# Attention 0 of a two-layer transformer block: half of its unmasked maximum scans split into a half of the scores and a clipped difference

## The reference, cut to what matters

```python
q = apply_rope(q, 0)                      # 32 heads of 16 features
k = apply_rope(k, 0)                      # 8 key heads, each shared by 4 query heads
scores = jnp.einsum('bhqd,bhkd->bhqk', q, k) / math.sqrt(HEAD_DIM)
scores = jnp.where(causal[None, None, :, :], scores, jnp.float32(-1e+20))
attn = jax.nn.softmax(scores, axis=-1)
out = jnp.einsum('bhqk,bhkd->bhqd', attn, v)
```

## Time and profile before

| | us |
|---|---|
| median of 3 executions (lowest, highest) | 1353.01 (1350.63, 1364.93) |
| profiled execution, its own time | 1344.81 |
| its span | 1343.1 |
| TensorE busy | 1205.7 |
| VectorE busy | 953.5 |
| ScalarE busy | 671.2 |
| GpSimd busy | 375.2 |

### The profile page before, as it was taken

One profiled execution on the slowest core, in us unless ns is written; L12 is line 12 of the kernel. 1 busy time (PEld: TensorE's weight loads), 2 busy tenths in 40 slices (PEclk: granted clock), 3 DMA queues, 4 the chain that ended last, 5 costly groups with the idle time before them and its releaser, 6 DMA issues.

```text
span 1343.1 us, 21792 instructions
## 1 busy us (share of the span) xinstructions
PE 1205.7 (90%) x6800; PEld 753.2 (56%) x6800; DVE 953.5 (71%) x2990; ACT 671.2 (50%) x1023; POOL 375.2 (28%) x505
## 2 busy tenths in 40 slices
PE   4998999999899877998879999999988988879988
PEld 1875444443388865444868744444435887744368
DVE  5889889898166676653659798999962667576365
ACT  2621666666655452544436036666665554435542
POOL 0431411122254400114614323122213542002162
PEclk9996899999999997999979858999999999869999
DMA  8374411220010020100140742112200100120001
GB/s 317 120 196 87 125 29 26 57 65 3 1 49 1 1 47 19 55 2 0 63 175 23 189 130 70 26 26 57 66 2 0 50 1 17 32 72 2 1 8 56
DMA packets 37285, 76.20 MB, mean 57 GB/s; under 512 B 5084, under 2 KB 6620, under 8 KB 37036
## 3 DMA queue, kind: packets, MB, share of 16 engines
q1 hardware_dynamic: 37176, 74.82, 19.2%
HBM read 48.98 MB, written 27.08 MB: 57 GB/s over the span
## 4 chain that ended last, share of the span: by engine, by line
PE 64%; DVE 19%; issue 5%; POOL 5%; ACT 5%; DMA 1%; DVEq 0%; SPq 0%; ACTq 0%; POOLq 0%
PE bank L999 16%; PE bank L871 12%; PE bank L779 5%; PE bank L780 5%; PE bank L781 5%; DVE maxes L1208 5%; PE bank L983 4%; PE bank L977 3%; DVE unused L1204 3%; PE bank L765 3%; DVE ops L1152 3%; PE bank L881 2%; POOL x L1484 2%; POOL w_odd L1466 2%; ACT ops L1356 2%
## 5 line engine op out<-in xcount | busy, mean ns | idle before, releaser
L1431 ACT ACTIVATE probs<-bank 128x1024 f32<-128x1024 f32 (+3 forms) x416 | 367.9, 911 | 320.4 <-PE bank L983 220.3
L871 PE MATMUL bank<-ops 48*128 48x512 f32 (+3 forms) x960 | 321.8, 436 | 34.5 <-DVE maxes L1204 17.2
L1204 DVE CUSTOM_DVE_ANT_0 unused<-bank,causal 128x128 bf16<-128x128 f32 (+3 forms) x640 | 279.5, 486 | 47.7 <-PE bank L871 44.1
L1542 POOL TENSOR_SCALAR_AFFINE_SELECT probs<-probs 128x256 f32<-128x256 f32 (+1 forms) x256 | 118.8, 464 | 640.3 <-ACT probs L1431 640.0
L871 PEld LDWEIGHTS bank<-ops 48*128 48x128 f32 (+1 forms) x960 | 163.0, 206 | 218.9 <-DVE maxes L1204 96.0
L999 PE MATMUL bank<-probs,v_mem 128*17 128x512 f32 (+6 forms) x1920 | 252.2, 517 | 6.1 <-ACT heads_raw L1418 5.6
L1208 DVE TENSOR_REDUCE maxes<-bank 128x1 f32<-128x512 f32 x320 | 207.4, 684 | 40.7 <-PE bank L871 39.2
L983 PE MATMUL bank<-ops 50*128 50x512 f32 (+2 forms) x640 | 175.9, 448 | 5.0 <-ACT probs L1431 4.8
L779 PE MATMUL bank<-ops,xT 128*128 128x512 f32 (+1 forms) x288 | 116.2, 403 | 19.6 <-DVE x L1068 11.6
L983 PEld LDWEIGHTS bank<-ops 50*128 50x128 f32 x640 | 86.6, 197 | 57.9 <-ACT probs L1431 29.5
L1473 POOL TENSOR_TENSOR rstd<-var_eps,minus_half 128x1 f32<-128x1 f32 x96 | 52.7, 549 | 215.1 <-DVE var_eps L1046 214.5
(11 more groups left out here) (117 smaller groups left out, 1965.5 us busy)
## 6 DMA issues: line engine op xcount, KB each, us to landing
query_rows_dram<-ops SPq DMA_DIRECT2D x48, 256.0 KB, 3.8
ops<-query_rows_dram SPq DMA_DIRECT2D x64, 192.0 KB, 4.4
w_odd<-staging_wqkv SPq DMA_DIRECT2D x4, 1536.0 KB, 7.3
x<-x_dram SPq DMA_DIRECT2D x16, 256.0 KB, 6.1
ops<-ops SPq DMA_DIRECT2D x16, 256.0 KB, 3.0
out_dram<-x SPq DMA_DIRECT2D x16, 256.0 KB, 2.0
staging_wqkv<-wqkv_dram SPq DMA_DIRECT2D x2, 1536.0 KB, 15.8
key_rows_dram<-ops SPq DMA_DIRECT2D x24, 128.0 KB
```

The costliest lines, as they stand in the source:

```text
L871: last = mm(dst[:, h * w:(h + 1) * w], queries(a, u)[rows, t // 4, hi, t % 4 * P:(t % 4 + 1) * P], keys(a, u, hi)[rows, HALF * kp:HALF * k ...
L1204: V.tensor_tensor_reduce(unused[:, masked % 3, 0:w], part, causal[:, HALF - w:], 1.0, NEG, ALU.add, ALU.max, dst).then_inc(s["max_done"].s ...
L1431: A.activation(probs[:, e % 6, :, 0:cols], scores[:, 2 * (e % 2):2 * (e % 2) + 2, 0:cols], ACT.Exp, scale=a.scale).then_inc(s["exp"].sem, 1)
L1542: G.affine_select(out=p, in_=p, compare_op=ALU.is_ge, fill=0.0, base=0, pattern=pattern, channel_multiplier=-1).then_inc(s["masked"].sem, 1)
```

## The change

For the eight unmasked banks of a unit that belong to the first query block (`i` 0) the bank no longer holds the scores of 512 keys. Its left 256 columns hold the scores of keys 0 to 255, its right 256 columns the product with the difference of key rows, keys 256 to 511 minus keys 0 to 255. ScalarE clips the right half at zero (Relu) into one of three buffers `over`, and VectorE adds it to the left half and takes the maximum in one `tensor_tensor_reduce` of 256 columns, since max(a, b) = a + relu(b - a). The other eight unmasked banks keep their reduction of 512 columns.

Around this, the banks of a query tile are put in another order; an instruction on VectorE writes the differences into lanes 64 to 127 of the first key products, which are then stored with them (128 lanes in place of 64; the high and low parts are still made of 64 lanes); two transfers load them; TensorE waits for them ahead of such a bank; and `xT` moves into the tail of `ops` to make room. The buffers of `over` are those of `hw_mem` and `v_rest`, which the attention does not use.

```diff
+        if self.row_tiles == 2:
+
+            for t in range(4, NT):
+                at = [n for n, m in enumerate(self.max_banks) if m[0] == t]
+                first, second = ([self.max_banks[n] for n in at if self.max_banks[n][1] == kp] for kp in range(2))
+                half = len(second) // 2
+                self.max_banks[at[0]:at[-1] + 1] = first[:2] + second[:half] + first[2:] + second[half:]
...
+        self.halved = [n for n, (t, kp, w, g, diag) in enumerate(self.max_banks) if not diag and self.row_tiles == 2 and g[0][1] == 0]
...
-        xT = sb("xT", [P, 2, 2, KC, P], F32R)
-        ops = sb("ops", [P, 20, SEQ], F32R)
+        ops = sb("ops", [P, 22, SEQ], F32R)
...
+        over = [hw_mem[:, 0:2, :], hw_mem[:, 2:4, :], v_rest]
...
+            if n == 0:
+                last.then_inc(s["summed"].sem, 1)
+                eng.wait_ge(s["summed"].sem, s["summed"].at(b, 1))
+                half = HALF // 2
+                last = ops_of.tensor_tensor(prods[64:P, 0:2, 0:half], prods[0:64, 0:2, half:], prods[0:64, 0:2, 0:half], ALU.subtract)
+            last.then_inc(s["turned"].sem, 1)
...
+            def load_key_differences(b):
+                sp.wait_ge(rope_stored[0].sem, rope_stored[0].at(b, 96))
+                for r in range(2):
+                    dst = ops_flat[64 * r:64 * r + A0.part_rows, 20480:21504].bitcast(F32).rearrange("p (n s) -> p n s", n=4)
+                    sp.dma_start(dst, k_rows[8:16].rearrange("(n r) p s -> r p n s", r=2)[r, :, :, 0:HALF // 2]
+                                 ).then_inc(key_differences_done.sem, 16)
...
+                    if g == 0:
+                        load_key_differences(b)
...
+                    if n in a.halved:
+                        r, hi = heads_in[0]
+                        pe.wait_ge(key_differences_done.sem, key_differences_done.at(b, 32))
+                        rows = a.score_rows(r, a.part_rows)
+                        last = mm(dst.rearrange("p (n s) -> p n s", n=2), queries(a, u)[rows, 1, hi, t % 4 * P:(t % 4 + 1) * P],
+                                  halved_keys(u // 2)[rows], start=True, stop=True)
...
+                        elif n in a.halved:
+                            k = a.over_at[i]
+                            dve.wait_ge(s["over"].sem, s["over"].at(b, k + 1))
+                            V.tensor_tensor_reduce(unused[:, paired % 3, 0:w // 2], src[:, 0:w // 2],
+                                                   over[k % 3].rearrange("p n c -> p (n c)"), 1.0, NEG,
+                                                   ALU.add, ALU.max, dst).then_inc(s["max_done"].sem, 1)
+                            paired += 1
...
+            def clip_difference(b, st, i):
+                a, s = ATT[st], qs[st]
+                act.wait_ge(s["ring_full"].sem, s["ring_full"].at(b, i + 1))
+                A.activation(over[a.over_at[i] % 3].rearrange("p n c -> p (n c)"), ring[i % 3][:, HALF // 2:], ACT.Relu
+                             ).then_inc(s["over"].sem, 1)
...
                         for n, (_, cols) in enumerate(a.events[k_]):
                             e = u * a.unit_events + a.events_before[k_] + n
+                            if n == 1:
+                                clip_differences(ring_no + len(a.ring_at[g][0]))
                             act.wait_ge(s["scored"].sem, s["scored"].at(b, e + 1))
...
+                    clip_differences(len(a.ring_first) + sum(len(slot) for step in a.ring_at[:g + 1] for slot in step))
```

More of the change, by code:

```diff
@@ L133, in plan_max @@
                 self.max_banks += [(t, kp, w, g, diag) for g in groups]
+        if self.row_tiles == 2:
[5 more added lines that the diff above has]
+        self.halved = [n for n, (t, kp, w, g, diag) in enumerate(self.max_banks) if not diag and self.row_tiles == 2 and g[0][1] == 0]
         self.max_ops_to = list(itertools.accumulate(len(m[3]) for m in self.max_banks))
         self.unit_max_ops = self.max_ops_to[-1]
-        ops = [m[4] for m in self.max_banks for _ in m[3]]
-        self.masked_ops = [n for n, diag in enumerate(ops) if diag]
+        self.paired = [m[4] or n in self.halved for n, m in enumerate(self.max_banks)]
+        ops = [pair for m, pair in zip(self.max_banks, self.paired) for _ in m[3]]
+        self.paired_ops = [n for n, pair in enumerate(ops) if pair]
         self.max_banks_of = [sum(m[0] < 4 for m in self.max_banks), len(self.max_banks)]
@@ L235, in plan_ring @@
         self.norm_at = [i for i, item in enumerate(self.ring) if item[0] == "norm"]
+        self.over_at = {i: n for n, i in enumerate(i for i, item in enumerate(self.ring)
+                                                   if item[0] == "max" and item[2] in self.halved)}
 A0 = Attention("rot", 32, 8, 16, 0.25, 2, True, ahead=1.07, slack=12)
@@ L380, in build @@
         ops_flat = ops.rearrange("p n s -> p (n s)")
+        xT = ops_flat[:, 20480:22528].rearrange("p (m n k c) -> p m n k c", m=2, n=2, k=KC)
         regions = {"E": [ops_flat[:, 0:2048], ops_flat[:, 2048:4096]],
@@ L408, in keys, with halved_keys @@
             return ops_flat[:, first:first + 1024]
+        def halved_keys(v):
+            first, second = 64 + 4 * v, 80 + v
+            return ops_flat.rearrange("p (n s) -> p n s", s=HALF // 2)[:, first:second + 1:second - first, :]
         def all_keys(a):
@@ L442, in build @@
         keys_first_done = signal("first_keys_loaded", 32)
+        key_differences_done = signal("key_differences_loaded", 32)
         keys_second_done = signal("second_keys_loaded", 32)
@@ L488, in build @@
             s["turnable"] = signal(f"{n}_rope_products", 6)
+            s["summed"] = signal(f"{n}_first_keys_roped", 1)
             s["turned"] = signal(f"{n}_roped", 6)
@@ L496, in build @@
             s["max_done"] = signal(f"{n}_max_done", a.units * a.unit_max_ops)
+            s["over"] = signal(f"{n}_differences_clipped", a.units * len(a.halved))
             s["shift_step"] = signal(f"{n}_shift_step", 3 * a.units)
@@ L529, in rope_sums @@
             ops_of.tensor_tensor(prods[0:m, 0, :], prods[0:m, 0, :], prods[0:m, 3, :], ALU.subtract)
-            ops_of.tensor_tensor(prods[0:m, 1, :], prods[0:m, 1, :], prods[0:m, 2, :], ALU.add).then_inc(s["turned"].sem, 1)
+            last = ops_of.tensor_tensor(prods[0:m, 1, :], prods[0:m, 1, :], prods[0:m, 2, :], ALU.add)
+            if n == 0:
[4 more added lines that the diff above has]
+            last.then_inc(s["turned"].sem, 1)
         def queries_count(u):
@@ L542, in build @@
         rope_lanes = [64, P, 64, P, P, P]
+        stored_lanes = [P, P, 64, P, P, P]
         @block.sync
@@ L612, in store_rope @@
                 _, hi, lo = rope_set(n % 2)
-                lanes, rows = (64, k_rows) if keys_only else (P, q_rows[16 * (n // 4):16 * (n // 4) + 16])
+                lanes = stored_lanes[n]
+                rows = k_rows[0:lanes // 8] if keys_only else q_rows[16 * (n // 4):16 * (n // 4) + 16]
                 rows = rows.rearrange("h (p m d) s -> p m h d s", p=3, m=2)
@@ L868, in ring_item @@
                     operands_ready(b, st, u, t)
-                    for h, (r, hi) in enumerate(heads_in):
+                    if n in a.halved:
[4 more added lines that the diff above has]
+                                  halved_keys(u // 2)[rows], start=True, stop=True)
+                    for h, (r, hi) in enumerate(heads_in if n not in a.halved else ()):
                         rows = a.score_rows(r, a.part_rows)
@@ L1193, in ring_read @@
                     t, kp, w, heads_in, diag = a.max_banks[n]
-                    masked = u * len(a.masked_ops) + sum(len(m[3]) for m in a.max_banks[:n] if m[4])
+                    paired = u * len(a.paired_ops) + sum(len(m[3]) for m, pair in zip(a.max_banks[:n], a.paired) if pair)
                     for h, head in enumerate(heads_in):
@@ L1408, in attention, with clip_differences @@
                 ns = len(a.steps)
+                ring_no = max(a.begun.values())
+                def clip_differences(upto):
+                    nonlocal ring_no
+                    for i in range(ring_no, upto):
+                        if i in a.over_at:
+                            clip_difference(b, st, i)
+                    ring_no = upto
+                clip_differences(len(a.ring_first))
                 for g in range(a.units * ns + a.lag + 2):
@@ L1594 @@
     rows = [nc.dram_tensor(f"{n}_dram", shape, F32, kind="Internal").ap()
-            for n, shape in (("key_rows", (8, 48, SEQ)), ("query_rows", (32, 48, SEQ)))]
+            for n, shape in (("key_rows", (16, 48, SEQ)), ("query_rows", (32, 48, SEQ)))]
     build(nc, w.pop("x"), w, scratch, *rows, out)
```

13 lines of the change are left out of this document (6 added, 7 removed).

## The result

The changed kernel took 1443.02 us (median of 4 executions, 1439.76 to 1452.41); the kernel before, run beside it, 1355.36. The ratio is 1.0649, with a 95% interval of 1.0567 to 1.0730. The prediction was 1376 with a range to 1400: the sign was right, the size was not.

The account below looks back on a forecast made before the run. VectorE was taken to pace the ring. The profiled 1344.8 us plus 25.5 for late clips, minus 4.0 in the burst, plus 1.5 for the subtraction gave 1367.8; the same +23.0 on the median 1353.0 gave 1376 us, range 1338 to 1400.

Parts of the forecast that it names:

- What bounds the kernel: First attention, steady units: VectorE sets the ring's pace, working 26.29 of 28.26 us; it holds up TensorE, which holds up ScalarE.
- its warning: In one unit the chain of waits lies on VectorE for only 19.9%, mostly on TensorE's own queue; the margin is thin.
- the lower bound of 1322 us: Every clip is in time and only the saving of 2.0 us per unit counts: -30.5 us in all.
- The scan's spacing: VectorE's new 256-column scans start 0.35 us apart against 0.60 for plain reductions: 0.25 us saved per bank, 2.0 per unit.
- Lateness of the clips: Tiles 4 to 7: eight clips late by 5.13 us per unit; less saving and absorbed waits, +1.82 net, 14 units +25.5.
- the 1.31 us of old waits: VectorE's present waits for TensorE, 1.97 us per unit less 0.66 already counted, that can vanish into the stalls for clips.
- The stores at nothing: Storing 128 lanes and two more loads cost nothing, since tile 4 already waits for the second keys; otherwise some us per sequence.
- The burst at -4.0: First unit's eight halved banks per sequence, in the burst and step 0 with ScalarE nearly idle: 16 x 0.25 us saved.
- a rival at 0.13 and at 33 us: Steady units: TensorE standing for clips is granted a lower clock, one spell of 2.37 us per unit, 1409 us; chance 0.13.
- Clips in time: Rival: full banks ahead of VectorE hide the path through ScalarE, only the saving counts, 1322 us; chance 0.15.
- A draw: Rival: half the lateness is hidden or stalls fall where the chain lies on TensorE, about 1353 us; chance 0.22.
- The rule that relu belongs on VectorE: A skill's rule against the clip on ScalarE; relu as a second VectorE pass was put at +13 us, 1366 us.

Follow-up runs that it names:

- free scan: Changed kernel without clips or waits for them; VectorE scans the left 256 columns with zero mask columns, clipped half left out: 1339.25 us, ratio 0.9876.
- clips in the burst alone: Changed kernel with the old bank order and only the six banks per sequence ahead of the first step halved and clipped: 1353.43 us, ratio 1.0003.
- no clips: Changed kernel without ScalarE's clips and VectorE's wait for them, VectorE reducing all 512 columns; new order, difference matmuls and transfers stay: 1394.61 us, ratio 1.0284.

## Why the prediction was wrong in size

**What bounds the kernel: right, with its warning.** VectorE is the pace of the ring. The free scan shows what relief of it is worth: 0.8 us per unit for 1.75 us of work. My sum gave relief its full 2.0 us, and the lower bound of 1322 us with it.

**The scan's spacing: right, where it doesn't wait.** The new scan takes 425 ns, and neighbours start 0.35 us apart, with a float32 second operand as with the mask:

```profile
115.41 0.42 DVE L1255 CUSTOM_DVE_ANT_0 unused<-bank,hw_mem 128x256 bf16<-128x256 f32 x1 [0.33 <-ACT hw_mem L1461]
...
115.76 0.42 DVE L1255 CUSTOM_DVE_ANT_0 unused<-bank,hw_mem 128x256 bf16<-128x256 f32 x1
```

In the units, where each waits, VectorE's work fell by 1.4 us and not by 2.0.

**Lateness of the clips: right in kind, a third too small.** The two clips of tile 7 and the first of tile 4 waited 0.67, 0.76 and 0.69 us where 0.60, 0.86 and 0.63 were worked out. The last of tile 6 waited 1.39 where I "took 0.1": the step failed in that I looked only at what stands ahead of the clip on ScalarE, not at the value matmuls ahead of its bank. Together they are 7.76 against 5.13, and 2.29 of the 2.63 more fall on tiles 5 and 6, at the low clock. The net at full clock was 2.3 us per unit against 1.82, 14 x 0.5 = 7 us more in all. That the net came so near is in part luck: the lateness was larger, the work saved was less, and more than the 1.31 us of old waits was absorbed. Without the clock's 12 x 4.3 = 52 us the profiled execution would have taken some 1394 us against the 1367.8 of my sum, and these 26 us are the 7 and the places outside the steady units.

**The stores at nothing: perhaps wrong by some 2 us.** In the chain of waits after, ahead of the first ring matmul, stands a transfer where the kernel before shows none:

```profile
83.35 4.24 DMA query_rows_dram<-ops
...
87.96 6.50 DMA ops<-query_rows_dram
```

The first ring matmul, before the change and after:

```profile
91.63 0.44 PE L871 MATMUL bank<-ops 48*128 48x128 f32 x4
```

```profile
94.59 0.53 PE L917 MATMUL bank<-ops 48*128 48x128 f32 x4 [0.59 <-DMA ops<-query_rows_dram]
```

It is 3.0 us late. With the same stores it came at 92.40 (clips in the burst alone), 92.75 (free scan) and 94.08 (no clips), and in the kernel before with doubled matmuls in the burst, which has neither the subtraction nor the stores, at 92.42. So of the 3.0 us about 1 is the spread of traces, and up to 2 may be the stores in sequence 0. The cover I named (tile 4 waits anyway) was the wrong place to look: the queries of the first tiles are loaded behind these stores.

**The burst at -4.0: it gave nothing back.** The row of six units begins 9.4 us late in sequence 0 (167.5 for 158.1), with a clock of 0.53 from 106 to 140 us where it had been 0.60. By the same rows the 101 us are 9.4 ahead of the six units of sequence 0, 38.6 in them, 9.4 from there to the six of sequence 1, 41.0 in those and 2.8 behind. What of the 21.6 us outside is clock and what stalls wasn't worked out.

**The step that failed: the clock stood at nothing in the sum, held as a rival at 0.13 and at 33 us, where it was the larger half.** I argued from the end of the attention, where TensorE has less to do and keeps 1.00, that a TensorE that stands more keeps its clock. The runs say otherwise where VectorE holds it up: low clock per unit was 0.6 to 1.7 us before, 13.4 after, 10 with VectorE's scans of the halved banks doubled, and about 10 with only 1.2 us of work added. The rival had the form right, one spell of low clock in each unit; it took the spell of 6.7 us seen before, and it was 10 to 17 us. Twelve units at 0.35 x 12 us are some 50 us of the 80, the rest the stalls. Both were in my text; they are not rivals but add up, and the traces tie the one to the other: the clock falls right behind the two late clips of tile 4. The Trainium skill (TensorE: Matmul & The Clock Gate, section "A second HAM failure mode: psum-queue depth-cycling") describes a case like this, with bf16 matmuls of 512 columns: a TensorE that idles briefly and often while it cycles through PSUM banks goes back and forth between its two clocks. The trace agrees in that, with a fall and a rise in each unit and 0.81 on average in a ring of three banks. The same skill (Trainium Kernel Development and Optimization, section "Performance Expectations") calls matmul busy time a bad metric for how close a kernel is to the roofline. The trace agrees: it rose from 167.85 to 195.40 us in six units on 1156 matmuls each.

**The rivals.** Clips in time: refuted, each waits. A draw: refuted, the kernel lost 88 us. The rule that relu belongs on VectorE stayed on the right side in sign, as the clip on ScalarE made the kernel slower than before; relu on VectorE, for which I worked out 1366 us, wasn't tried, so whether it beats either is open.

**What stays open.** What in the stands brings the clock down. Standing is not the whole of it: in the kernel before the clock fell at 232.5 us behind 4 us in which TensorE was busy for 3.90, more than at tile 4, where it kept its clock.

```profile
228.50:232.50 4.00, 3.90 (x29) 2.04 (x31) 4.00 (x17) 3.76 (x5) 0.00 (x0) 1.00 0.03 6
232.50:236.50 4.00, 4.00 (x17) 1.55 (x9) 3.02 (x8) 1.54 (x2) 0.00 (x0) 0.50 0.00 0
```

The order of banks alone gave 0.91 and 0.90 in its two rows of six units, with the difference matmuls and transfers 0.89 and 0.83, at nearly one pace; the free scan, with those same matmuls, 0.98. Whether the second step is the operands or chance wasn't separated, nor why these two, with VectorE's work as before, had so much more low clock than the kernel before.

No version that computes the whole result was faster than the kernel before. The free scan was, by 1.2%, but it leaves out the clipped half.

## What to carry to other kernels

Before work is split to relieve an engine, trace the longer way it takes through the queue of the helper: here a clip of 0.39 us behind an exponential of 1.03 kept VectorE waiting for 0.85 us on average, though the helper was busy for half of the span, and a ring of three banks did not hide it. Where TensorE is fed through such a ring, price each added stall with the clock it may bring down: here 2.3 us of stall became 6.6. And look at the granted clock per unit of the steady part before and after every change: this kernel lost 1.0% by the reordering of equal work.

## What the runs showed of the hardware

The price of the low clock, in us of time per microsecond at the lower level, differed from kernel to kernel. It was 0.35 in the kernel before (28.26 against 30.63) and with the new order (28.40 against 32.00), 0.36 in the changed kernel (34.14 against 36.53), 0.28 with 1.2 us of scans added (28.80 against 32.70), and 0.11 with 4.8 us of scans added (33.82 against 34.88), where VectorE works for over 30 us of each unit. Only the free scan, with the least work for VectorE, comes nearer to the half that matmuls alone would lose between 2.4 and 1.2 GHz: 0.42 (27.46 against 30.24, 6.7 us low). That the slack of the slower engine covers the slow matmuls is my reading; no run tests it.

An added load of 1.2 us per unit on VectorE, 4% of its work, took 13.7 us of one unit to the low clock; 16 added matmuls per unit took some of it back (0.81 to 0.89). In the changed kernel the clock fell at the same place of each unit of the steady part, right behind the late clips of tile 4, and the longest stand of TensorE there was 1.1 us (at 248.01, for VectorE).
